# A macaron layer (expert layer, gated delta-rule attention, expert layer) on one core: expert sums by products with weight diagonals, first projections by batches, key and query norms by products with ones

## The reference

```python
x = x + 0.5 * ffn(layernorm(x))          # 16 experts, top 4 of them for a token, and a shared expert
x = x + attn(layernorm(x))               # 16 heads, DK = DV = 128
x = x + 0.5 * ffn(layernorm(x))

# ffn: softmax scores, top-4 weights normed to sum 1;
#   y = sum over the 4 experts of weight * (silu(x Wg) * (x Wu)) Wd, plus the shared expert
# attn, for each head:
q, k, v = silu(conv4(x Wq)), silu(conv4(x Wk)), silu(conv4(x Wv))
v_hat = k Wsv^T ; e = v_hat - v
s = [sqrt(sum e^2), sum |e|, 1 - sum(v_hat v) / (|v_hat| |v|)]
beta = sigmoid(mlp(s)) ; amp = mlp(s)
g = -exp(A_log) * softplus(k / |k| * amp + dt_bias)
qn, kn = q / |q|, k / |k|
S_t = exp(g_t) S_{t-1} + kn_t (v_t - kn_t exp(g_t) S_{t-1}) beta_t ; o_t = qn_t S_t
o = rmsnorm(o) * norm_w * sigmoid(gate(x)) ; out = o Wo
```

## Time and profile before

| what | value |
|---|---|
| median of 3 runs | 1574.29 us (1563.8 to 1580.26) |
| the profiled execution | 1571.55 us, its span 1569.7 us |
| busy: PE, DVE, ACT, POOL | 1360.0, 1060.1, 807.1, 687.8 us |
| TensorE clock, mean granted | 0.940 of full speed |

### The profile page before, as it was taken

How to read it: one execution, slowest core, us unless ns; L and a number is a source line. 1 busy time by engine, 2 the same in 40 slices (tenths; PEclk the granted TensorE clock), 3 DMA queues, 4 the chain that set the end, 5 groups by cost and what they waited for, 6 DMA issues and landing times.

```text
span 1569.7 us, 28651 instructions
## 1 busy us (share of the span) xinstructions
PE 1360.0 (87%) x9424; PEld 1050.0 (67%) x9424; DVE 1060.1 (68%) x1981; ACT 807.1 (51%) x2597; POOL 687.8 (44%) x991
## 2 busy tenths in 40 slices
PE   7999757778989889898898898898977889899993
PEld 5777524557767767777676676687766667757772
DVE  5744366778868778889788888897774621265445
ACT  1122127576776766867767668678574332011220
POOL 0277700355354452554644535535455430005772
PEclk9899967899999999999999999999988989989997
DMA  9233320011120220211211311111013213242334
GB/s 359 61 104 103 115 99 20 16 43 34 36 61 17 56 71 15 58 30 46 67 32 31 84 30 32 45 48 51 17 46 110 88 46 148 103 209 71 105 102 174
DMA packets 130960, 117.04 MB, mean 75 GB/s; under 512 B 58944, under 2 KB 115328, under 8 KB 130048
## 3 DMA queue, kind: packets, MB, share of 16 engines
q1 hardware_dynamic: 121216, 90.20, 18.2%
q0 software_dynamic: 9024, 24.65, 5.4%
q10 hardware_dynamic: 576, 0.34, 0.1%
HBM read 80.30 MB, written 34.87 MB: 73 GB/s over the span
## 4 chain that ended last, share of the span: by engine, by line
PE 67%; DVE 15%; ACT 6%; issue 5%; DMA 3%; POOL 2%; DVEq 0%; SPq 0%; POOLq 0%; ACTq 0%
PE proj L1241 9%; DVE big L2829 6%; PE chain L556 5%; PE low L1383 5%; PE tree L1383 5%; PE gates L534 4%; PE low L534 3%; PE proj L1281 2%; PE proj L1287 2%; PE chain L1469 2%; PE tree L1427 2%; PE proj L1515 2%; PE tree L1452 2%; PE proj L471 2%; DVE x L903 2%
## 5 line engine op out<-in xcount | busy, mean ns | idle before, releaser
L3549 POOL TENSOR_TENSOR big<-big 128x512 f32<-128x512 f32 (+6 forms) x112 | 60.4, 539 | 378.2 <-PE tree L1392 123.5
L2829 DVE SCALAR_TENSOR_TENSOR big<-proj,pall,big 128x1022 f32<-128x1022 f32 x129 | 164.4, 1274 | 13.9 <-ACT big L2109 7.8
L1241 PE MATMUL proj<-xT,wqkv 128*128 128x512 f32 x344 | 158.8, 605 | 16.3 <-DVE big L2829 15.6
L2985 DVE TENSOR_TENSOR KQ<-KQ,big 128x1024 f32<-128x1024 f32 x112 | 150.3, 1342 | 17.3 <-PE low L1355 8.3
L980 POOL DMA_INDIRECT inv<-xn_scr,gidx x94 | 91.3, 971 | 135.2 <-DVE sidx L841 107.1
L3551 POOL TENSOR_TENSOR big<-big 128x512 f32<-128x512 f32 x112 | 145.4, 1298 | 0.0
L1241 PEld LDWEIGHTS proj<-xT,wqkv 128*128 128x128 f32 x344 | 63.2, 194 | 82.8 <-issue 63.1
L986 POOL DMA_INDIRECT y_scr<-inv,sidx x94 | 92.8, 987 | 37.0 <-issue 22.5
L626 ACT COPY big<-proj 128x256 f32<-128x256 f32 x94 | 35.2, 374 | 125.9 <-PE proj L523 125.8
L3563 POOL TENSOR_TENSOR prodw<-D,W 64x15 f32<-64x15 f32 (+7 forms) x240 | 89.4, 373 | 18.8
L1383 PE MATMUL low<-KQ,big 128*128 128x128 f32 x640 | 91.1, 286 | 7.6 <-POOL big L3551 4.0
(11 more groups left out here) (311 smaller groups left out, 3649.2 us busy)
## 6 DMA issues: line engine op xcount, KB each, us to landing
big<-in_w_ex SPq DMA_DIRECT2D x2, 4864.0 KB, 20.8
big<-in_w_ex SPq DMA_DIRECT2D x2, 4256.0 KB, 18.7
big<-y_scr SPq DMA_DIRECT2D x8, 1024.0 KB, 8.2
m_img<-big SPq DMA_DIRECT2D x16, 512.0 KB, 3.2
inv<-t_img SPq DMA_DIRECT2D x16, 512.0 KB, 4.2
big<-t_img SPq DMA_DIRECT2D x16, 512.0 KB, 5.1
o_scr<-obuf SPq DMA_DIRECT2D x15, 512.0 KB, 4.0
wqkv<-in_wqkv SPq DMA_DIRECT2D x16, 384.0 KB, 3.8
```

Of the source, the lines that this page charges most:

```text
L1241: m = te.matmul(place(h, j)[:, b, :], wqkv[:, h % 2, j, k, :], xT[:, k, b * T:(b + 1) * T], start=(k == 0), stop=(k == KB - 1))
L2829: ve.scalar_tensor_tensor(conv[:, :, d:T], place(h, j)[:, :, 0:T - d], pall[:, h, 4 * j + 3 - d:4 * j + 4 - d], conv[:, :, d:T], ALU.mult, ...
L2985: ve.tensor_tensor(kr, kr, dl, ALU.mult).then_inc(mkq.sem, 1)
```

## The change

**Expert sums.** ACT makes, between its steps for the blocks, 32 diagonal matrices of 128x128 from the identity and a column of `wk` (`weight_diagonal`, into `hotA`). PE then forms each quarter of the sum as 8 products of such a diagonal with 128x256 rows of `y4`, in PSUM (`expert_sums`), and DVE adds the quarter to `x` in one operation of 128x512. This holds for both expert layers.

**First projections.** Head 0's projections run batch by batch: `first_batch` needs only the first half of `xT` and stands ahead of the transposes of the third and fourth quarter. The gate's product (`gate_rows`) stands behind head 0's projections, in other banks; ACT copies it between `tap_v(0)` and `silu_k(0)`.

**Norms.** `k_sq` and `q_sq` are now one square each of 128x1024 in SBUF, straight behind the silu of k and further on for q. `p_norms` replaces `p_kk` and `p_qq`: 16 products with a block of squares as weights and 4 columns of ones as moving operand. ACT copies their results to `kq2` (`norms_out`). Beside this, ACT copies v_hat to SBUF (`v_guess_rows`), `err` reads the copy, and `vhat_sq` squares it in place after `err`.

```diff
+            def weight_diagonal(r):
+                m = se.activation(hotA[r // TB][:, r % TB, :], ident[:, :], ACT.Copy, scale=wk[:, r:r + 1])
...
+            def expert_sums(q):
+                te.wait_ge(*y_sum.of(f, 1))
+                te.wait_ge(s_x[q], 16 + 16 * (f + 1))
+                for i in range(2):
+                    n = 2 * q + i
+                    for k in range(TOPK):
+                        t = te.matmul(bank[q][:, i * H:(i + 1) * H], hotA[k][:, n, :], y4[:, n, k, :], start=(k == 0),
+                                      stop=(k == TOPK - 1))
...
             def expert_sum(q):
...
-                        m = ve.scalar_tensor_tensor(x[:, n, :], y4[:, n, k, :], wk[:, k * TB + n:k * TB + n + 1], x[:, n, :],
-                                                    ALU.mult, ALU.add)
...
+                ve.tensor_tensor(rows, rows, bank[q], ALU.add).then_inc(x_up, 1)
...
             @live
-            def p_kk(h):
-                te.wait_ge(*silu.of(h, 1))
-                te.wait_ge(*prod.of(h))
-                to_rows(cvk[:, h % 2, :], kk)
-
-            @live
-            def p_qq(h):
-                te.wait_ge(*silu.of(h, 3))
-                te.wait_ge(*ksq.of(h, 1))
-                to_rows(cvq[:, h % 2, :], kk)
+            def p_norms(h):
+                te.wait_ge(*vh2.of(h, 1))
+                te.wait_ge(*ksq.of(h, 2))
+                for i, squares in enumerate((k_squares, q_squares)):
+                    for c in range(BN):
+                        at = 4 * (i * BN + c)
+                        m = te.matmul(FF[:, 0, at:at + 4], squares[:, c * P:(c + 1) * P], ones[:, :], start=True, stop=True)
+                m.then_inc(kk.sem, 1)
...
             def begin():
+                first_batch()
+                layernorm_te(te, 1, 2)
+                layernorm_te(te, 1, 3)
                 p_k(0)
                 p_v(0)
                 p_q(0)
+                gate_rows()
...
+            def v_guess_rows(h):
+                se.wait_ge(*vhat.of(h))
+                se.wait_ge(*v2.of(h - 1))
+                se.copy(wide(v_guess), FF[:, :, :]).then_inc(vh2.sem, 1)
...
             def vhat_sq(h):
-                se.wait_ge(*vhat.of(h))
+                se.wait_ge(*prod.of(h))
...
+                se.activation(k_squares, cvk[:, h % 2, :], ACT.Square).then_inc(ksq.sem, 1)
...
+                se.activation(q_squares, cvq[:, h % 2, :], ACT.Square).then_inc(ksq.sem, 1)
```

More of the change, by code:

```diff
@@ L1553, in begin @@
                 p_v(1)
-                p_kk(0)
-                p_qq(0)
+                p_norms(0)
                 p_q(1)
@@ L1570, in begin @@
                 t_diag(0, 0)
-                p_qq(1)
+                p_norms(1)
                 t_lvl(0, 0, 1)
@@ L1605, in begin @@
                 i_tr(0, 1, 4)
-                p_qq(2)
+                p_norms(2)
                 i_tx(0, 0, 5)
@@ L1676, in turn @@
                 c_oT(t - 4, 1)
-                p_qq(t - 1)
+                p_norms(t - 1)
                 i_tx(t - 3, 1, 5)
@@ L1752, in finish @@
                 i_ty(11, 5)
-                p_qq(13)
+                p_norms(13)
                 t_diag(12, 0)
@@ L1817, in finish @@
                 i_tr(12, 0, 4)
-                p_qq(14)
+                p_norms(14)
                 i_tr(12, 1, 4)
@@ L1893, in finish @@
                 t_diag(14, 1)
-                p_qq(15)
+                p_norms(15)
                 c_oT(12, 0)
@@ L2097, in attention_se, with gate_rows @@
             se.wait_ge(s_scr, 16)
-            for n in range(TOK // 512):
-                se.wait_ge(g1_mm, n + 1)
-                se.copy(g1[:, n * 512:(n + 1) * 512], bank[n]).then_inc(g1_s, 1)
+            def gate_rows():
+                for n in range(TOK // 512):
+                    se.wait_ge(g1_mm, n + 1)
+                    se.copy(g1[:, n * 512:(n + 1) * 512], bank[2 + n]).then_inc(g1_s, 1)
             def wide(v):
@@ L2359, in begin @@
                 tap_v(1)
-                k_sq(0)
+                q_sq(0)
                 e_sq(0)
-                q_sq(0)
+                norms_out(0)
                 exp_set(0)
@@ L2369, in begin @@
                 silu_k(1)
+                k_sq(1)
                 silu_v(1)
@@ L2441, in turn @@
                 i_trs(t - 4, 0, 4)
-                k_sq(t - 2)
+                q_sq(t - 2)
                 i_trs(t - 4, 1, 4)
+                vhat_sq(t - 2)
                 v_sq(t - 2)
-                q_sq(t - 2)
+                norms_out(t - 2)
                 x_ev(t - 4, 5)
@@ L2463, in finish @@
                 silu_k(12)
+                k_sq(12)
                 exp_set(0)
@@ L2504, in finish @@
                 i_trs(10, 0, 4)
-                k_sq(12)
+                q_sq(12)
                 i_trs(10, 1, 4)
+                vhat_sq(12)
                 v_sq(12)
-                q_sq(12)
+                norms_out(12)
                 e_sq(12)
@@ L2522, in finish @@
                 silu_k(13)
+                k_sq(13)
                 c_us(10, 0, 0)
@@ L2565, in finish @@
                 i_trs(11, 1, 4)
-                k_sq(13)
+                q_sq(13)
                 x_ev(11, 5)
                 o_pow(10)
+                vhat_sq(13)
                 v_sq(13)
-                q_sq(13)
+                norms_out(13)
                 i_trs(11, 0, 5)
@@ L2587, in finish @@
                 silu_k(14)
+                k_sq(14)
                 c_us(11, 0, 0)
@@ L2624, in finish @@
                 x_ev(12, 4)
+                vhat_sq(14)
                 v_sq(14)
-                k_sq(14)
+                q_sq(14)
                 decay(13)
@@ L2687, in finish @@
                 decay(14)
+                vhat_sq(15)
                 v_sq(15)
@@ L2693, in finish @@
                 i_trs(13, 1, 4)
-                k_sq(15)
+                q_sq(15)
                 e_sq(15)
-                q_sq(15)
+                norms_out(15)
                 powers(15)
```

164 lines of the change are left out of this document (89 added, 75 removed).

## The result

The changed kernel takes 1654.65 us in the median of 4 runs (1647.58 to 1658.13), against 1572.36 (1563.8 to 1580.26) for the kernel before: slower by 5.2%, ratio 1.0524 [1.0489, 1.0558]. The forecast of 1608 had the direction, and its range (to 1625) did not hold the time. One execution of a later experiment, `e12`, took 2119.72 us at a mean clock of 0.631, where its other three had 0.945, and is in none of the ratios.

The account below looks back on a forecast made before the run. PE, busy 87% of the span, was taken as the bound. To the profiled 1571.55 us came 3.5 (norms), 24 (clock), 4.6 (second layer's sums) and 3 (start): 1606.7, forecast as 1608, range 1570 to 1625.

Parts of the forecast that it names:

- norms at full clock, in the turns: Attention heads 2 to 15: the new norms' cost without clock falls, +3.5 us, from -10 to +11.
- clock in the turns: Attention heads: clock falls brought by `p_norms`, +24 us, from 0 to 39.
- start of the attention: First expert layer's sums through the first heads: norms' products wait for ACT's squares, +3 us, from -3 to +6.
- second layer's sums: End of the second expert layer: PE's sums take 17.0 us against 12.4, +4.6, bounds +2.1 and +16.
- Norms, in one turn: Turn from 809 us: 16 thin products take 3.16 us against 1.04 for 8 transposes, shorter waits offset most; +0.25 a turn.
- costs 1 us a head where that cover is gone: Last head: `k_sq` delays two `c_us` on ACT, without PE's 1.8 us of `t_lvl` ahead of `c_ko`; 1 us.
- Norms and the clock: Attention: the thin run of `p_norms` brings the clock down in 12 of 14 heads, +24 us.
- I take 2.0: Price in us of one clock fall behind `p_norms`, chosen from 0.9 to 2.8 seen in earlier turns.
- that half-clock case: Attention start: norms' products run at half clock after 6 us of idle PE, `g_sT(0)` at 267 against 261.3 before.
- The first projections: Attention start: `p_k(0)` ends near 222.7 in place of 227.2, 4.5 us early, but ACT does not pass it on.
- The clock did not keep up: Rival for the attention: `p_norms` is too short to bring the clock down; 1582.7 us, 1576 to 1592; chance 33%.
- Falls that last: Rival: clock stays low until each head's projection and throughout the second layer's sums; 1636 us; chance 10%.

Follow-up runs that it names:

- e12: The changed kernel with 64 columns of ones, the products on squares of k ahead of `i_ty`, and ACT reordered in the end heads: 1596.36 us, ratio 1.0158.
- e3: The changed kernel with 64 columns of ones in place of 4 in the norms' products: 1623.28 us, ratio 1.0314.
- e5: The kernel before, with the 8 transposes of k (`p_kk`) made twice in heads 2 to 15: 1573.27 us, ratio 1.0033.
- e9: The kernel before, with 16 products of 4 columns of ones added behind `c_oT` in heads 2 to 15: 1657.64 us, ratio 1.0541.
- e11: The kernel before, with 32 transposes added behind `c_oT` in heads 2 to 15: 1614.31 us, ratio 1.0295.
- e4: The kernel before, with only the expert sums changed, in both layers: 1574.17 us, ratio 1.0011.
- e2: The kernel before, with expert sums and first projections changed but norms as before: 1574.38 us, ratio 1.0021.

## Why the prediction was wrong

| term | forecast | measured |
|---|---|---|
| norms at full clock, in the turns | +3.5 | +21.2 |
| clock in the turns | +24 | +44.4 |
| start of the attention | +3 | +11.9 |
| second layer's sums | +4.6 | +3.8 |
| sum | 35.1 | 81.3 |

The first two rows share out 65.6 us, by a sum that counts a fall in full also where it lies over a wait. e3 is a check on it: with 20 us less lost to the clock its turns come to 930.3 us at full clock, 16.6 over the kernel before, so 21.2 may be read as 17 to 21.

**Norms, in one turn: mis-sized.** +0.25 us a turn was +1.19. Of the 0.94 between them 0.4 is the price of a product with 4 columns, which I took from four in a row at 0.198 and which is 0.223 in a run of 16. The rest is `i_tr`: I counted the removed `p_kk` as 1 us gained, with `i_tr` at 843.05, 2.48 us after the start of `i_ty`. The way from `i_ty` through DVE to `i_tr` takes 3.15, so most of `p_kk` had been hidden, and e5 shows the same from the other side. 1.19 in twelve turns would be 14 us. Turn by turn, with the clock's loss taken off, the first twelve are 8.4 us longer and the last three 12.8, 7.6 of it in the long turn. For those I had "costs 1 us a head where that cover is gone" and nothing else: there `g_norm` waits 2.2 us for DVE and `p_norms` 1.5 for ACT, which now square and subtract in another order.

**Norms and the clock: right mechanism, half the size.** e9 to e11 show the mechanism alone, without ACT's and DVE's part of the change. "Falls here in most heads, 12 of 14" was right in kind: it was 10 of 14. Two steps failed. The first is "I take 2.0": the ten falls lose 3.1 us each, 31 in all in place of 24, and one in e9 costs 3.2. I had capped it at 2.8 by a turn of the earlier trace rows whose fall lies where PE is idle in part (1.60 and 1.31 of 2 us busy at 517 and 519 us), so that not all of it was paid. The second is that the sum had falls nowhere else: the other falls lose 41 us in place of 28, and these 13 to 14 us were in no term. Five of them begin 2 to 3.3 us behind the start of `i_ty`, where the kernel before has none up to 1150 us. All five stand at a wait of some 0.8 us ahead of `i_tr`, and in four of them PE had waited 1.0 to 1.9 us ahead of `i_ty` too (0.80 and 1.32 in the turn from 816 us): the change had made a wait out of the cover that it took away. That these falls come from the waits was seen in the trace only, and not tested by itself.

The Trainium skill ("TensorE: Matmul & The Clock Gate", Part 1 on the clock gate) has the clock follow how busy PE was. In e9 PE is busy 2.00 of 2 us and goes to half clock, and in e11 it is as busy and stays at 1.00, so busy time as the profile counts it does not decide. The same page's remark on transposes (Part 4), that they don't count as busy in the same way, is not borne out here: 32 of them in a row, in float32, kept 1.00.

**Start: half clock left out, and half of it not looked at.** The forecast of `p_k(0)` by 223, of the norms' products at 256.0 and of `g_sT(0)` at 267 at half clock all came within 1.2 us; `g_sT(0)` is 6.5 later than before. I chose +3 in place of that half-clock case (+6), though PE had stood idle for 6 us ahead. The other 5.4 us lie between `g_sT(0)` and the first `i_ty`, for which the prediction has no term; `p_norms(1)` is there with 4.65 us.

**Sums: right.** The chain's end took 16.6 us of the forecast 17.0. e4 puts all sums at +1.7 us [-1.4, 4.9], e2 sums and projections at +3.3. The first projections gave nothing, as forecast.

**The rivals.** The clock did not keep up. "Falls that last", 1636, was nearer than the forecast: its 39 us for the clock in the turns compare with 44.4 and its 6 at the start with 11.9, but the 16 for the sums at half clock did not come, and the price of the norms at full clock, 3.5 there too, made up for them.

## What to carry to other kernels

A product with few moving columns is not a cheap product: with a run of 16 the clock fell, full products behind it that had nothing to do with it ran at half clock, and that cost another 3.2 us, and sixteen times the columns came out 31 us faster. Before counting a removed operation as a gain, follow what starts next: where another engine's answer is awaited there, the removed work was cover, and what goes in its place is a wait, here in five turns with a fall of the clock behind it. When two effects of a change are priced, price a fall of the clock by half the length of the stretch at half clock under work that doesn't pause, not by turns in which it lay over waits.

## What the runs showed of the hardware

Of three runs that take 3.5 us each at full clock, behind the same 0.63 us of wait, those of 4 columns lost 52.6 us more to the clock over 14 heads than 32 transposes did (a fall in or right behind the run in 14 of 14 heads, against none), and those of 64 columns 14.4 more (one head). 16 products take 3.5 us at 4 as at 64 columns (3.56 and 3.59 us to the start of what follows), so narrower ones save nothing. And the kernel with transposes added lost less to the clock than the kernel before without them, 18.1 us against 28.0; one profiled execution of each shows this, the mean clocks of all their executions overlap (0.942 to 0.951 against 0.939 to 0.949), and no run was made to explain it.
